# An attention loop's output product moved to another PSUM bank, and its step laid out anew on all engines

## The reference, cut to what matters

```python
x = x + _L0_attn_ref(_layernorm(x, axis=-1), w_q, w_k, w_v, w_o)
...
q = (hidden_states @ w_q).reshape(B, S, H, Dh)          # S 2048, H 16, Dh 64
k = (hidden_states @ w_k).reshape(B, S, H, Dh)
v = (hidden_states @ w_v).reshape(B, S, H, Dh)
mask = dilated_mask(S)      # own segment of 64, and every 4th position up to 256 away
scores = jnp.einsum('bqhd,bkhd->bhqk', q, k) * scaling + mask[None, None]
attn = jax.nn.softmax(scores.astype(jnp.float32), axis=-1)
out = jnp.einsum('bhqk,bkhd->bqhd', attn, v).reshape(B, S, H * Dh)
return out @ w_o
```

## Time and profile before

| what | value |
|---|---|
| median of 3 runs | 467.33 us (466.6 to 468.13) |
| profiled execution: span | 468.2 us |
| PE busy | 443.3 us, 95% |
| DVE, ACT, POOL busy | 84%, 71%, 63% |
| attention's loop on PE | about 59 to 303 us |

### The profile page before, as it was taken

How to read it: one execution, slowest core, us unless ns; L and a number is a source line. 1 busy time by engine, 2 the same in 40 slices (tenths; PEclk the granted TensorE clock), 3 DMA queues, 4 the chain that set the end, 5 groups by cost and what they waited for, 6 DMA issues and landing times.

```text
span 468.2 us, 17264 instructions
## 1 busy us (share of the span) xinstructions
PE 443.3 (95%) x6440; PEld 348.8 (74%) x6440; DVE 394.1 (84%) x1344; ACT 333.0 (71%) x975; POOL 296.5 (63%) x491
## 2 busy tenths in 40 slices
PE   7999699999999999999999899998987989999996
PEld 5687588888888888888787678887744757558775
DVE  5888598997988899799797697996899989998775
ACT  3678668778768777877786678695566579987533
POOL 4222576687576768667865587665669897674322
PEclk9999999999999999999999999999999999999999
DMA  6477952356345335445455564464000000000003
GB/s 224 175 254 201 276 122 53 75 115 123 75 84 110 74 74 109 81 78 109 86 116 122 110 135 90 77 123 91 1 1 0 0 2 0 2 0 2 1 0 91
DMA packets 136098, 40.53 MB, mean 87 GB/s; under 512 B 104976, under 2 KB 131024, under 8 KB 136016
## 3 DMA queue, kind: packets, MB, share of 16 engines
q1 hardware_dynamic: 135440, 38.38, 35.9%
q10 hardware_dynamic: 576, 1.05, 0.6%
HBM read 29.44 MB, written 9.96 MB: 84 GB/s over the span
## 4 chain that ended last, share of the span: by engine, by line
PE 59%; POOL 9%; DMA 8%; DVE 8%; ACT 7%; SPq 4%; issue 3%; ACTq 0%; POOLq 0%; DVEq 0%
PE psum L464 10%; PE psum L422 10%; PE psum L484 5%; PE psum L1186 5%; PE psum L498 5%; PE psum L495 4%; PE psum L510 4%; PE psum L403 4%; DMA st<-w_rows_dram 3%; DMA w_rows_dram<-st 3%; PE psum L1181 3%; ACT pband L569 3%; PE psum L405 2%; PE psum L404 2%; POOL area L1827 2%
## 5 line engine op out<-in xcount | busy, mean ns | idle before, releaser
L948 POOL TENSOR_SCALAR pband<-pband,fac 128x192 f32<-128x192 f32 x256 | 103.9, 424 | 84.8 <-DVE fac L771 84.7
L569 ACT ACTIVATE pband<-pband,st 128x192 f32<-128x192 f32 x256 | 113.2, 448 | 0.9 <-DVE st L719 0.9
L719 DVE CUSTOM_DVE_ANT_0 pband<-psum,band_mask 128x192 f32<-128x192 f32 x256 | 76.0, 353 | 0.1
L422 PE MATMUL psum<-keys,q_class 64*64 64x192 f32 (+2 forms) x1536 | 66.3, 274 | 0.0
L464 PEld LDWEIGHTS psum<-ident,pband 128*128 128x128 f32 x384 | 45.3, 141 | 25.5 <-issue 17.8
L464 PE MATMUL psum<-ident,pband 128*128 128x128 f32 x384 | 53.1, 273 | 6.1 <-DVE arena L836 3.1
L422 PEld LDWEIGHTS psum<-keys,q_class 64*64 64x64 f32 x1536 | 57.7, 133 | 1.4 <-issue 1.4
L569 ACT ACTIVATION_READ_ACCUMULATOR pband<-pband,st 128x1 f32 x256 | 49.5, 193 | 0.0
L938 POOL COPY q_class<-q_rows 128x512 f32<-128x512 f32 x32 | 36.4, 1137 | 14.0 <-ACT q_rows L609 14.0
L930 POOL COPY keys<-k_rows 128x512 f32<-128x512 f32 x32 | 36.2, 1131 | 14.3 <-issue 7.2
L780 DVE COPY pt<-psum 128x512 f32<-128x512 f32 x64 | 43.6, 682 | 0.4
(11 more groups left out here) (213 smaller groups left out, 1086.4 us busy)
## 6 DMA issues: line engine op xcount, KB each, us to landing
v_rows_dram<-arena SPq DMA_DIRECT2D x32, 256.0 KB, 4.6
v_both<-v_rows_dram SPq DMA_DIRECT2D x32, 256.0 KB, 3.9
v_seg<-v_rows_dram SPq DMA_DIRECT2D x64, 128.0 KB, 3.8
v_side<-v_rows_dram SPq DMA_DIRECT2D x96, 64.0 KB, 2.6
w_rows_dram<-st SPq DMA_DIRECT2D x64, 8.0 KB, 3.0
st<-w_rows_dram SPq DMA_DIRECT2D x64, 8.0 KB, 2.5
arena<-_attn_hidden_states_dram SPq DMA_DIRECT2D x4, 256.0 KB, 3.9
out_dram<-x SPq DMA_DIRECT2D x4, 256.0 KB, 2.5
```

Source lines behind the costliest of these rows:

```text
L422: return pe.matmul(bank[2 * r + head][rows, at:at + y.shape[1]], x, y, start=True, stop=True, skip_group_check=True)
L569: act.activation(x, x, ACT.Exp, bias=mine[:, head:head + 1], scale=-1.0, accum_out=mine[:, 2 + head:3 + head]).then_inc(s_exp, 1)
L719: dve.tensor_tensor_reduce(pband[:, G % P_SLOTS, c, head, :], bank[2 * r + head][:, at:at + BAND], band_mask[:, (0, 1, 1, 2)[w], SEG * (1 ...
L948: pool.tensor_scalar(x, x, fac[:, F % 2, 1, c, head:head + 1], 1.0, ALU.mult, ALU.mult).then_inc(s_scaled, 1)
```

## The change

`output(U)` now writes `out_bank` (bank 6), from which ACT has just copied the weighed values. `accumulate` reads bank 6, `weigh(U, 0)` waits for `s_acc` (the accumulation of the unit before) in place of `s_out`, and bank 7 has two occupants per step in place of three. The step is laid out anew on every engine, and the pipeline on PE is one step longer (scores are taken for `t - 3`, not `t - 2`). Prologue and the first calls of the closing list follow. SP's order is the same.

```diff
-        return {"key": (s_key, x + 1), "query": (s_query, x + 1), "wo": (s_acc, x + 1)}[name]
+        return {"key": (s_key, x + 1), "query": (s_query, x + 1)}[name]
...
                 if b == 0:
-                    wait(pe, s_out, U)
+                    wait(pe, s_acc, U)
...
-                wait_shared(pe, U, "wo")
                 pe.wait_ge(s_out, U + 1)
-                pe.matmul(shared_bank[:, :], wo[:, U // NW, :], o_sb[:, :], start=True, stop=True).then_inc(s_mix, 1)
+                pe.matmul(out_bank[:, :], wo[:, U // NW, :], o_sb[:, :], start=True, stop=True).then_inc(s_mix, 1)
...
             for t in range(FIRST_STEP, DRAIN):          # PE
+                scores(t - 3, 0)
+                weigh(t - 7, 2)
+                scores(t - 3, 1)
+                weigh(t - 7, 3)
+                turn(t - 6, 0)
+                project(t - 1, 0)
+                turn(t - 6, 1)
+                output(t - 7)
                 project(t, 1)
+                turn(t - 6, 2)
+                turn(t - 6, 3)
                 weigh(t - 6, 0)
                 weigh(t - 6, 1)
-                turn(t - 6, 3)
-                output(t - 7)
-                turn(t - 5, 0)
-                weigh(t - 6, 2)
-                scores(t - 2, 0)
-                weigh(t - 6, 3)
-                scores(t - 2, 1)
-                project(t, 0)
-                turn(t - 5, 1)
-                turn(t - 5, 2)
...
             for t in range(FIRST_STEP, DRAIN):          # ACT (two conditional lines left out)
-                exp_difference(t - 4)
                 take_out(t - 6)
                 take_queries(t)
                 odd_turned(t - 5, 1)
+                seg_exps(t - 2)
+                exp_difference(t - 4)
+                band_exps(t - 2, 1)
                 take_keys(t + 1)
-                band_exps(t - 2, 0)
                 odd_turned(t - 5, 3)
-                seg_exps(t - 2)
-                band_exps(t - 2, 1)
+                band_exps(t - 1, 0)
...
             for t in range(FIRST_STEP, DRAIN):          # DVE (conditional lines left out)
-                differences(t - 4)
-                even_turned(t - 5, 0)
-                factors(t - 4)
+                factors(t - 5)
+                seg_sums(t - 3)
                 band_max(t - 2, 0)
                 seg_max(t - 2, 0)
-                even_turned(t - 5, 2)
                 seg_max(t - 2, 1)
+                differences(t - 4)
+                even_turned(t - 5, 0)
                 band_max(t - 2, 1)
-                seg_sums(t - 2)
                 accumulate(t - 6)
+                even_turned(t - 5, 2)
...
             for t in range(FIRST_STEP, DRAIN):          # POOL (its index runs 3 ahead of before)
-                scale_band(t - 5, 1)
-                keys_by_class(t)
-                scale_seg(t - 5)
-                scale_band(t - 4, 0)
-                queries_by_class(t - 1)
+                scale_band(t - 8, 1)
+                scale_seg(t - 8)
+                keys_by_class(t - 3)
+                queries_by_class(t - 4)
+                scale_band(t - 7, 0)
```

More of the change, by code:

```diff
@@ L226, in shared_reader @@
     def shared_reader(x, name):
-        return {"key": (s_key, x + 1), "query": (s_query, x + 1), "wo": (s_acc, x + 1)}[name]
[L231 to L236, removed]
+        return {"key": (s_key, x + 1), "query": (s_query, x + 1)}[name]
+    kinds = {"k": "key", "q": "query", "o": "wo"}
+    occupants = [(int(x[1:]), kinds[x[0]]) for x in (
+        "k0 k1 q0 k2 q1 k3 q2 k4 q3 k5 q4").split()]
+    for t in range(FIRST_STEP, DRAIN):
+        occupants += [(t - lag, who) for who, lag in (("query", 1), ("key", 0))
+                      if there(t - lag) and (t - lag, who) not in occupants]
+    occupants += [(x, who) for x, who in ()]
     def wait_shared(pe, x, name):
@@ L516, in _ @@
[L516 to L520, removed]
@@ L521, in _ @@
-            values(28); project(4, 0); values(29); values(30); project(5, 0); values(31); turn(0, 0); scores(3, 1)
-            turn(0, 1); turn(0, 2)
-            for t in range(FIRST_STEP, DRAIN):
+            keep_busy(7); turn_rows(0); keep_busy(4); values(0); values(1); values(2); project(0, 1); turn_rows(1)
+            values(3); project(1, 1); values(4); values(5); turn_rows(2); values(6); project(0, 0); values(7)
+            values(8); project(2, 1); values(9); values(10); turn_rows(3); scores(0, 0); scores(0, 1); values(11)
@@ L542, in _ @@
              trx, op, t5, fc0, fc1, fc2, fc3, pr, t6, k, r, kv) = tail_tensor(pe)
-            output(26); turn(27, 3); weigh(27, 0); weigh(27, 1); weigh(27, 2); scores(31, 0); weigh(27, 3)
-            scores(31, 1); turn(28, 0); turn(28, 1); output(27); turn(28, 2); turn(28, 3); weigh(28, 0); weigh(28, 1)
+            scores(30, 0); weigh(26, 2); scores(30, 1); weigh(26, 3); turn(27, 0); turn(27, 1); output(26)
+            turn(27, 3); turn(27, 2); scores(31, 0); scores(31, 1); weigh(27, 0); weigh(27, 1); weigh(27, 2)
@@ L545, in _ @@
+            weigh(27, 3); turn(28, 0); turn(28, 1); output(27); turn(28, 2); turn(28, 3); weigh(28, 0); weigh(28, 1)
             weigh(28, 2); weigh(28, 3); turn_weights(0); turn_weights(1); turn(29, 0); output(28); turn_weights(2)
@@ L901, in _ @@
              xr, k1, k2, o0, o) = tail_vector(dve)
-            differences(29); band_max(31, 0); factors(29); even_turned(28, 0); seg_max(31, 0); seg_max(31, 1)
-            even_turned(28, 2); band_max(31, 1); accumulate(27); seg_sums(31); differences(30); clear()
-            even_turned(29, 0); accumulate(28); factors(30); x1(0); bn0(0); ag0(0); even_turned(29, 2)
-            differences(31); qx0(0); qx1(0); qx2(0); even_turned(30, 0); factors(31); accumulate(29)
-            even_turned(30, 2); qx7(0); qx8(0); x1(1); xq(0); bn0(1); ag0(1); even_turned(31, 0); xqt(0)
@@ L912, in _ @@
[L912 to L916 removed]
+            factors(28); seg_sums(30); band_max(31, 0); seg_max(31, 0); seg_max(31, 1); differences(29)
@@ new lines, in _ @@
+            even_turned(28, 0); band_max(31, 1); accumulate(27); factors(29); even_turned(28, 2); seg_sums(31)
+            differences(30); clear(); even_turned(29, 0); accumulate(28); factors(30); x1(0); bn0(0); ag0(0)
+            even_turned(29, 2); differences(31); qx0(0); qx1(0); qx2(0); even_turned(30, 0); factors(31)
+            accumulate(29); even_turned(30, 2); qx7(0); qx8(0); x1(1); xq(0); bn0(1); ag0(1); even_turned(31, 0)
+            xqt(0); accumulate(30); even_turned(31, 2); qx0(1); qx2(1); x1(2); hm0(0); bn0(2); ag0(2); qx7(1); qx8(1)
@@ L1020 @@
+            rs3(2); rs3(3); rs4(0); rs4(1); shift_weights(); rs4(2); rs4(3); o(1); o(0)
 STEPS = {
```

151 lines of the change are left out of this document (77 added, 74 removed), and 16 rows, old and new, of the table STEPS.

## The result

The changed kernel takes **503.48 us** (median of 4 runs, 503.33 to 508.0) beside 467.73 us for the kernel before on the same chip: ratio 1.076, 95% interval 1.070 to 1.082. I had forecast 468.6, range 463.5 to 471.5. The forecast is wrong by 35 us.

The account below looks back on a forecast made before the run. PE's own chain of work was taken to bound the loop, with DVE next at 88%. The terms +4.0 + 1.7 - 3.0 - 1.6 + 0.2 = +1.3 us on 467.3 gave 468.6 us, range 463.5 to 471.5.

Parts of the forecast that it names:

- term 2: Loop: statistics get 3 to 4 us more time, so PE's 1.63 us wait at 268.38 goes: -1.6 us, at worst 0.
- term 5: `weigh(U, 0)` waiting for `accumulate` through bank 6: hidden in the loop, a cost behind the attention's last units: +0.2 us.
- Term 1: PE's loop: one change of tile size less per step, 0.12 us in each of 25 steps: -3.0 us.
- test of 8.66 us: PE's short loop step, 8.80 us before, should take 8.66; the prediction fails if its length is not that.
- Term 3: Prologue: the load of `w_o` comes too late for `output(0)`; PE stands 5.6 us, kernel 4.0 us late there.
- Term 4: PE's clock falls after the 5.6 us idle, slowing the set of work behind the wait: +1.7 us.
- rival that the clock stays: PE keeps its clock through the wait for `w_o`, everything else as forecast: 466.9 us; chance 0.22.
- rival of a wait at bank 6: The way round bank 6 becomes a wait in every step, 6 us more: 474.6 us; chance 0.08.

Follow-up runs that it names:

- experiment 1: Changed kernel with `differences` moved behind `accumulate`, `seg_sums` ahead of `factors` (DVE) and `exp_difference` behind `band_exps` (ACT): 469.87 us, ratio 0.999 to the kernel before.
- experiment 2: Changed kernel with only DVE's `differences` moved behind `accumulate`: 473.18 us, ratio 1.003 to the kernel before.
- experiment 3: Changed kernel with DVE's two-operand subtraction replaced at its place by two reductions of one SBUF operand each: 471.16 us.
- experiment 4: Changed kernel with two small TENSOR_SCALARs added per step on POOL, ahead of the keys' and the queries' copies: 476.93 us, ratio 1.007 to the kernel before.
- experiment 10: experiment 1 with the load of `w_o` moved right behind `send_statistics(2)` on SP's queue: 462.29 us, ratio 0.984 to the kernel before.
- experiment 11: experiment 1 with 12 extra matmuls on PE ahead of the wait for `w_o`: 468.04 us, ratio 0.997 to the kernel before.

## Why the prediction was wrong, point by point

- **What failed: a move costed at nothing.** Of `differences` I priced only the wait in front of it (term 2) and gave its own duration no price at the new place. That price is up to 3 us of waiting for POOL in each step. DVE had 12% to spare in the loop, about 1.1 us in a step of 8.8; L750 takes 2.3 more in the median, DVE becomes the bound, and a step takes 1.1 us more than before in the mean, where I had forecast 0.12 less. Experiments 1 to 4 show it: other place, other operands or other neighbours on POOL take back 27 to 34 us. I had said that DVE's new order gives it slack ahead of the product (term 5); the opposite held. The sign was to be read in the trace of before, whose longest L754 took 1.366 us where 0.193 is usual: it began at 63.62, in POOL's copy of the keys, and ended 0.05 us after the `scale_seg` that followed.
- **Term 1, right in kind and too small.** A step has 8.53 to 8.55 or 9.00 us in the undisturbed stretches of experiments 1, 2 and 10, where the kernel before had 8.79 or 9.26: 0.25 us less, not 0.12, or -6.3 us for 25 steps in place of -3.0. The chain of work of experiment 1, one short step (136.70 to 145.25):

```profile
140.07 0.59 PE psum L465 x4
140.66 0.24 PE psum L404
140.89 0.23 PE psum L405
141.12 0.23 PE psum L406
...
142.65 0.23 PE psum L404
142.88 0.23 PE psum L405
143.12 0.24 PE psum L406
```

  Both projections take 0.70 where I had booked 0.77: their first matmul costs no more than the others, behind transposes too. My test of 8.66 us was off by the same 0.11, within rounding.
- **Term 2, right.** DVE idled 16.9 us in 8 places for the statistics before, 2.2 us in 3 after, and 1.0 in 2 in experiment 1.
- **Term 3, right.** Forecast 5.6 us of waiting, iteration 6 ended at 60.1; measured 5.37 and 59.96.
- **Term 4, right in kind; its size came out by luck.** The rival that the clock stays is refuted (experiment 11). The Trainium skill's "TensorE: Matmul & The Clock Gate", Part 1, which I had weighed there, said so, and the trace agrees: the mean granted clock is 0.59 over the 4.5 us behind the wait. I had booked +1.7 as half of a worst case of 3.5. The kernel after paid 1.8, but experiment 1, with nearly the same idle, paid 2.9. Terms 3 and 4 together: the set of work done at 70.42 is done at 75.88, +5.5 for the +5.7 booked.
- **Term 5, right without the port wait, wrong with it.** PE waits 11.2 us in 19 places for `accumulate` after, and 1.2 us in all in experiment 1. So my rival of a wait at bank 6 named a wait that exists, but not its source.
- **A term that I had not.** In some executions DVE, now that it is no longer held up, comes to the quantisation before `w_down` has landed. In the profile of experiment 1, DVE around 125 us, then POOL:

```profile
125.06 0.55 DVE L854 TENSOR_REDUCE q_scale<-arena 128x24 f32<-128x384 f32 x1 [3.18 <-DMA arena<-in_L_ffn_w_down_dram]
125.64 2.66 DVE L855 TENSOR_SCALAR q_scale<-q_scale 128x24 f32<-128x24 f32 x1
...
125.17 1.04 POOL L955 TENSOR_TENSOR pseg<-pseg,fac 128x512 f32<-128x512 f32 x1
126.16 1.08 POOL L928 COPY keys<-k_rows 128x512 f32<-128x512 f32 x1
127.19 1.08 POOL L936 COPY q_class<-q_rows 128x512 f32<-128x512 f32 x1
```

  The wait of 3.18 us pushes the next instruction, 0.21 us elsewhere, into POOL's string, where it takes 2.66. That step has 15.5 us in place of 9.0. The load took 5.0 us to land there. In experiment 11, with the same orders, it took 3.0 us, DVE did not wait, and the step has 9.00. In experiment 10 the load took 5.1 us, but the wait of 2.43 us met the string late (0.34 us) and the step lost 2.0. So this step is part of why experiment 1 spreads from 467.9 to 479.2 us; how many of its executions pay it is not known, and why the load's landing varies stays open.

Put together, each sum for one profiled execution against that of before. The parts are the loop (-6.3), the statistics (-1.6), the time at which the set done at 70.42 is done, and the step of `w_down`.

| profile | sum | measured |
|---|---|---|
| experiment 1, set done at 77.06 | -6.3 - 1.6 + 6.6 + 6.5 = +5.2 | +5.7 |
| experiment 11, 74.94 | -6.3 - 1.6 + 4.5 = -3.4 | -2.2 |
| experiment 10, 68.86 | -6.3 - 1.6 - 1.6 + 2.0 = -7.5 | -6.7 |

The profile of experiment 1 is one of its longest executions (475.84 us beside a median of 469.87). That my 468.6 stands close to that median is thus partly chance: the error of 3.3 in term 1 works against the slower clock and the missing term. What stays open is 0.5 to 1.2 us of these sums, and why DVE gets in beside TENSOR_SCALARs.

## What to carry to other kernels

When instructions are moved, look at what the other engine of a shared port does at the new time, not only at waits: a wait for the port has no row of its own, and shows only as a duration of one instruction far above its minimum, so read min, median and max of each small two-operand DVE instruction. Keep POOL's COPYs and TENSOR_TENSORs apart by a TENSOR_SCALAR, or DVE's two-operand instructions away from them; here the cheapest cure was one call moved. When one step gains pace, ask which loads were only just in time: two were, and moving the larger one earlier took the kernel from the time of before to 1.6% below it.

## What the runs showed of the hardware

- A DVE TENSOR_TENSOR with both operands in SBUF waits through POOL's whole string of COPY and TENSOR_TENSOR (2.55 us for three instructions), not just through the one that it meets. The Trainium skill, "SBUF — State Buffer", section "Who interferes with whom", has the pair of ports held for the whole instruction of the first; here POOL's next instruction, where it followed at once, came first in 22 of 25 cases.
- POOL's TENSOR_SCALAR on 128x192 in SBUF held DVE up by next to nothing: L750 took 0.20 us at 343.80, in the middle of eight of them, for 0.19. A TENSOR_SCALAR of 0.22 us is opening enough (experiment 4). The same section of the Trainium skill says that a GpSimd instruction which reads SBUF contends. It does here too, but POOL pays: beside DVE's longer instructions with two SBUF operands (0.57 to 0.71 us) its TENSOR_SCALAR of 0.43 us took 0.72 to 0.93, in all 14 such cases of the kernel after. Which of the two was issued first these rows do not tell; POOL's shows 0.01 us earlier:

```profile
159.67 0.80 POOL L946 TENSOR_SCALAR pband<-pband,fac 128x192 f32<-128x192 f32 x1
159.68 0.58 DVE L863 SCALAR_TENSOR_TENSOR arena<-arena 128x384 f32<-128x384 f32 x1
```

- DVE instructions with one SBUF operand, or with one in SBUF and one in PSUM, kept their times beside POOL's string: 0.17 us, and 0.42 for L729 (experiment 3). The exception is DVE's TENSOR_SCALAR from SBUF to SBUF, 2.66 us for 0.21 in experiment 1. The same section of the Trainium skill lists that operation among those that can take both ports.
